# A graph network and two attention rounds on one core: the last chunk's chain is spread over 24 slots in place of 12, one pair of blocks is taken later, and VectorE makes the chunk's mean and variance

## The reference, cut to what matters

```
h = max(layernorm(x), 0);  x = x + gnn(h, adj)      # hyperbolic graph network
h = max(layernorm(x), 0);  x = x + agnn(agnn(h))    # two attention rounds

gnn:   h1 = h_mul(h, embed), bias added;  neigh = exp0(adj @ log0(h1))
       out = h_mul(concat(h, neigh), layer), bias added
agnn(x):  s = beta * (xn @ xn.T), xn = x / |x|
          s = where(adj > 0, s, -1e9);  return leaky(softmax(s) @ x)
```

## Time and profile before

| | |
|---|---|
| median of three runs | 963.98 us |
| the profiled execution, its own time | 963.64 us |
| its span | 962.0 us |
| TensorE busy | 926.9 us, 96% |
| VectorE busy | 792.5 us, 82% |
| ScalarE busy | 538.0 us, 56% |
| granted TensorE clock, mean | 0.997 of full speed |

### The profile page before, as it was taken

One profiled execution on the slowest core, in us unless ns is written; L12 is line 12 of the kernel. 1 busy time (PEld: TensorE's weight loads), 2 busy tenths in 40 slices (PEclk: granted clock), 3 DMA queues, 4 the chain that ended last, 5 costly groups with the idle time before them and its releaser, 6 DMA issues.

```text
span 962.0 us, 22931 instructions
## 1 busy us (share of the span) xinstructions
PE 926.9 (96%) x9016; PEld 692.1 (72%) x9016; DVE 792.5 (82%) x1980; ACT 538.0 (56%) x867; POOL 7.2 (1%) x20
## 2 busy tenths in 40 slices
PE   7799999999997999999999999999999999999996
PEld 6644444444445878888888888778888888888886
DVE  7874778777789887978989898998788787888888
ACT  7802222232337766657656667796575565656564
POOL 0000000000000000000000000000000000000000
PEclk9999999999999999999999999999999999999998
DMA  8368888888851555455655545545455555565631
GB/s 298 154 222 289 283 298 293 279 286 283 293 180 57 232 196 210 186 202 198 249 195 212 220 180 216 210 160 201 177 219 219 232 206 201 220 228 194 259 144 37
DMA packets 30419, 207.26 MB, mean 215 GB/s; under 512 B 3632, under 2 KB 4784, under 8 KB 5744
## 3 DMA queue, kind: packets, MB, share of 16 engines
q1 hardware_dynamic: 28752, 203.70, 58.5%
q0 software_dynamic: 560, 1.84, 0.5%
q10 hardware_dynamic: 1008, 0.33, 0.1%
HBM read 203.75 MB, written 2.10 MB: 214 GB/s over the span
## 4 chain that ended last, share of the span: by engine, by line
PE 86%; ACT 6%; DVE 5%; issue 2%; DMA 0%; DVEq 0%; ACTq 0%
PE acc_ps L496 23%; PE s_ps L649 18%; PE s_ps L635 10%; PE acc_ps L707 6%; PE acc_ps L703 6%; PE acc_ps L705 6%; PE acc_ps L680 5%; PE acc_ps L676 5%; PE acc_ps L678 5%; ACT work L1078 1%; ACT set L800 1%; DVE work L1742 1%; PE s_ps L477 1%; ACT xt L822 1%; DVE work L1750 1%
## 5 line engine op out<-in xcount | busy, mean ns | idle before, releaser
L1078 ACT ACTIVATE work<-s_ps,beta_bias,beta_scale 128x1024 f32<-128x1024 f32 x144 | 173.5, 1205 | 212.2 <-PE s_ps L649 212.2
L496 PE MATMUL acc_ps<-ring,set 128*128 128x512 f32 x512 | 222.1, 592 | 1.6 <-DVE set L1348 1.6
L1760 DVE SCALAR_TENSOR_TENSOR h_all<-ring,s_ps 128x1024 f32<-128x1024 f32 x112 | 136.6, 1220 | 65.3 <-PE s_ps L635 63.9
L496 PEld LDWEIGHTS acc_ps<-ring,set 128*128 128x128 f32 x512 | 96.2, 190 | 117.5 <-issue 115.6
L1742 DVE TENSOR_TENSOR work<-work 128x1024 f16<-128x1024 f32 x96 | 132.7, 1382 | 5.4 <-ACT work L1088 5.4
L1088 ACT ACTIVATE work<-work 128x1024 f16<-128x1024 f32 x96 | 131.5, 1370 | 3.0
L1750 DVE SCALAR_TENSOR_TENSOR work<-ring,work 128x1024 f32<-128x1024 f32 x96 | 116.9, 1218 | 0.0
L649 PE MATMUL s_ps<-xt 128*128 128x512 f16 x432 | 105.4, 379 | 4.1 <-ACT work L1078 3.3
L649 PE MATMUL s_ps<-set 128*128 128x512 f16 x432 | 105.0, 379 | 0.5 <-ACT work L1078 0.5
L703 PE MATMUL acc_ps<-src,work 128*128 128x129 f16 x576 | 102.5, 219 | 2.0 <-DVE work L1750 2.0
L707 PE MATMUL acc_ps<-src,work 128*128 128x129 f16 x576 | 102.8, 222 | 0.0
(11 more groups left out here) (279 smaller groups left out, 1737.9 us busy)
## 6 DMA issues: line engine op xcount, KB each, us to landing
ring<-in_adj_t SPq DMA_DIRECT2D x192, 1024.0 KB, 5.0
x_sb<-in_x SPq DMA_DIRECT2D x4, 512.0 KB, 7.2
out<-x_sb POOLq DMA_DIRECT2D x7, 256.0 KB, 2.7
out<-x_sb SPq DMA_DIRECT2D x1, 256.0 KB, 2.7
w<-in_layer ACTq DMA_DIRECT2D x2, 64.0 KB, 8.2
w<-in_embed ACTq DMA_DIRECT2D x1, 64.0 KB, 4.5
eb<-in_embed_bias ACTq DMA_DIRECT2D x1, 64.0 KB, 6.9
lb<-in_layer_bias ACTq DMA_DIRECT2D x1, 64.0 KB, 7.9
```

Of the source, the lines that this page charges most:

```text
L496: last = nc.tensor.matmul(agg, v_sb[:, jb, :], ring[:, k, b, :], start=jb == 0, stop=jb == NB - 1)
L1078: nc.scalar.activation(values[x.n % VR], score_ps, ACT.Exp, bias=beta_bias[:, x.la:x.la + 1], scale=beta_scale[:, x.la:x.la + 1]).then_inc ...
L1760: V.scalar_tensor_tensor(turned[x.off % MR].rearrange("p (b j) -> p b j", b=CB), ring[:, x.mir_tile % AR, :, ds(x.h * HB * P, HB * P)], 0. ...
```

## The change

Four things are changed together:
- The order of round 0's halves. `half` is now made of segments: row 0 without its last pair (halves 0 to 13), row 1 (14 to 27), then the pair of chunks 0 and 7 as (a, b) = (7, 0) (28, 29), then rows 2 to 7. Row 0's own sums leave PSUM after half 13 into the free first part of `mirror_sums` (`own_kept`, ScalarE); the late pair's mirrored sum is added to them and its own sum goes to chunk 7's part (`late_total`, VectorE). Row 0 so ends with half 29, behind row 1 (half 27). Its tiny products stand in `mirrored_sum` of the late pair. Round 1's order stays.
- A pause does two slots in place of one: the chain lies over slots 1 to 24, chunk 7's columns are turned in slot 24 and first needed by half 26.
- The sums of rows in round 0 move from slots 4 to 8, 14 and 15 to slots 18 to 23 and 27.
- Mean and variance of the last chunk come from VectorE's statistics (`chunk_stats`, behind pause 7) in place of ScalarE's two passes (`chunk_variances`); ScalarE's rectified rows and squares (`chunk_relu`) are answered behind pause 8.

```diff
@@ -289,33 +289,69 @@
...
+        Seg = namedtuple("Seg", "first last row opens_after")
...
+        def add_seg(la, a, bs, row, opens_after):
+            first = len(half)
+            for b in bs:
+                own_tile = len(tile_of)
+                tile_of.append((b, a, len(half) + 1, None))
+                if b != a:
+                    tile_of.append((a, b, len(half) + 1, off_count[0] + 1))
+                for h in range(2):
+                    off = off_count[0] if b != a else None
+                    off_count[0] += b != a
+                    half.append(Half(la, a, b, h, len(half), off, off // 2 if b != a else None, len(segs),
+                                     own_tile, own_tile + 1))
+            segs.append(Seg(first, len(half) - 1, row, opens_after))
+            return segs[-1]
+        LATE = NC - 1
+        kept_seg = add_seg(0, 0, range(LATE), None, 0)
+        seg = add_seg(0, 1, range(1, NC), 0, 1)
+        rows_of.append(Row(0, 1, seg.first, seg.last))
+        late_seg = add_seg(0, LATE, (0,), None, 2)
+        rows_of.append(Row(0, 0, kept_seg.first, late_seg.last))
+        LATE_ROW = 1
+        for a in range(2, NC):
+            seg = add_seg(0, a, range(a, NC), a, a + 1)
+            rows_of.append(Row(0, a, seg.first, seg.last))
+        for a in range(NC):
+            seg = add_seg(1, a, range(a, NC), NC + a, NC + 1 + a)
+            rows_of.append(Row(1, a, seg.first, seg.last))
...
-        LAST_CHUNK_AT = 12
-        turned_at = {LAST_CHUNK_AT: (0, NC - 1), **{rows_of[a].last + (11 if a == 5 else 10): (1, a) for a in range(NC)}}
+        late_pair = half[late_seg.first].pair
+        def flushes_before(r):
+            return max([x.pair + 1 for x in half if x.off is not None and x.la == r.la and x.b == r.a], default=0)
+        def rows_summed_to(i):
+            return i + 1 - (i >= LATE_ROW)
+        def totals_to(i):
+            return i + 2
+        LAST_CHUNK_AT = 24
+        order_of = {(r.la, r.a): i for i, r in enumerate(rows_of)}
+        turned_at = {LAST_CHUNK_AT: (0, NC - 1), **{r.last + (11 if r.a == 5 else 10): (1, r.a) for r in rows_of[:NC]}}
...
-        SUMS_AT = 2 * NC - 1
-        SUMS_AT_OF = {4: (0, 1), 5: (2,), 6: (3,), 7: (4,), 8: (5,), 14: (6,), SUMS_AT: (7,)}
+        def turn_of(la, c):
+            return order_of[0, c] if la else c
+        SUMS_AT_LA = (rows_of[0].last, LAYER + 2 * NC - 1)
+        SUMS_AT_OF = {SUMS_AT_LA[0] - 11 + i: c for i, c in {2: (0, 1), 3: (2,), 4: (3,), 5: (4,), 6: (5,), 7: (6,),
+                                                             11: (7,)}.items()}
+        SUMS_AT_OF.update({LAYER + i: c for i, c in {4: (0, 1), 5: (2,), 6: (3,), 7: (4,), 8: (5,), 14: (6,),
+                                                     2 * NC - 1: (7,)}.items()})
@@ -640,8 +677,10 @@
...
                 wait(pe, raised, x.n)
-                if x.a == 0 and x.h == 0:
-                    pe.wait_ge(xt_lo[x.la], x.b + 1)
+                if x.la == 0 and x.h == 0 and (x.a == 0 or (x.a, x.b) == (1, NC - 1)):
+                    pe.wait_ge(xt_lo[0], x.b + 1)
+                elif x.a == 0 and x.h == 0:
+                    pe.wait_ge(xt_lo[1], max(x.b, LATE_ROW) + 1)
                 for u in range(HB):
@@ -678,7 +717,9 @@
...
                         last = nc.tensor.matmul(mir_ps[:, x.h, o], w[:, WORD_LO, col], src[x.la][:, q, F:AW],
-                                                start=False, stop=ib == CB - 1)
+                                                start=False, stop=ib == CB - 1 and x.pair != late_pair)
+                    if x.pair == late_pair:
+                        last = nc.tensor.matmul(mir_ps[:, x.h, o], tiny[:, :], sums_parts, start=False, stop=True)
                 last.then_inc(mir_added, 1)
@@ -686,20 +727,20 @@
...
-                r = rows_of[x.row]
+                seg = segs[x.seg]
                 pe.wait_ge(own_made, x.n + 1)
...
                     pe.wait_ge(consts_made, 9)
-                if x.n == r.first and x.row != LAST_ROW:
-                    wait(pe, total_made, x.row)
-                own_ps = own_of(x.row)
-                if x.n % LAYER == SUMS_AT - 2:
+                if x.n == seg.first and seg.row != LAST_ROW:
+                    wait(pe, total_made, seg.opens_after)
+                own_ps = own_of(seg.row)
+                if x.n + 2 in SUMS_AT_LA:
                     pe.wait_ge(sums_copied, x.la + 1)
...
                         col, q = ds(u * CH + ib * P, P), x.b * CB + x.h * HB + u
-                        opens = x.n == r.first and u == 0 and ib % 2 == 0
+                        opens = x.n == seg.first and u == 0 and ib % 2 == 0
                         nc.tensor.matmul(own_ps[:, ib // 2, ds(ib % 2 * PW, PW)], w[:, WORD_HI, col],
@@ -904,23 +945,12 @@
...
-            def chunk_variances():
+            def chunk_relu(c):
                 asked_for()
                 for b in range(CB):
-                    last = nc.scalar.activation(t2[:, b, :], t1[:, b, :], ACT.Copy, scale=-1.0 / F,
-                                                accum_out=small[:, 3, b:b + 1])
+                    last = nc.scalar.activation(t2[:, b, :], t1[:, b, :], ACT.Relu, bias=small[:, 3, b:b + 1])
                 last.then_inc(chunk_made, 1)
                 act.wait_ge(chunk_made, 1)
-                for b in range(CB):
-                    last = nc.scalar.activation(t3[:, b, :], t1[:, b, :], ACT.Square, bias=small[:, 3, b:b + 1],
-                                                accum_out=small[:, 2, b:b + 1])
-                last.then_inc(chunk_made, 1)
-            def chunk_relu(c):
-                for b in range(CB):
-                    last = nc.scalar.activation(t2[:, b, :], t1[:, b, :], ACT.Relu, bias=small[:, 3, b:b + 1])
-                last.then_inc(chunk_made, 1)
-                act.wait_ge(chunk_made, 3)
                 for b in range(CB):
@@ -965,10 +995,8 @@
...
                 on(ACT.Tanh, sm(5, CB), sm(4, CB))
-                for i in (6, 7):
+                for i in (6, 7, 8):
                     pause(i)
-                chunk_variances()
-                pause(8)
                 chunk_relu(c)
@@ -1092,16 +1120,22 @@
...
                 wait(act, flushed, x.pair)
-                wait(act, total_made, x.la * NC)
+                wait(act, total_made, x.la * (NC + 1))
                 nc.scalar.activation(mirror_sums[:, ds(x.b * CB, CB), :].rearrange("p (k b) w -> p k (b w)", k=2),
...
             def first_total(i):
-                act.wait_ge(row_summed, i + 1)
+                act.wait_ge(row_summed, rows_summed_to(i))
                 wait(act, inverse_made, i)
...
+            def own_kept():
+                act.wait_ge(own_added, kept_seg.last + 1)
+                nc.scalar.activation(mirror_sums[:, 0:CB, :].rearrange("p (k b) w -> p k (b w)", k=2), own_ps, ACT.Copy)\
+                    .then_inc(total_made, 1)
@@ -1152,13 +1186,16 @@
...
                 first = x and x.off is not None and x.h == 1 and x.a == 0
-                if i is not None and rows_of[i].a == 0:
+                own_leaves = n - 4 == kept_seg.last or (i is not None and i == NC)
+                if n - 4 == kept_seg.last:
+                    own_kept()
+                elif i == NC:
                     first_total(i)
...
                     raise_scores(at(n))
-                if i is not None and first:
+                if own_leaves and first:
                     first_flush(x)
@@ -1173,11 +1210,12 @@
...
-                slot(i + 1)
+                for n in range(SLOTS_PER_PAUSE * i + 1, SLOTS_PER_PAUSE * (i + 1) + 1):
+                    slot(n)
...
                 last_chunk(between)
-                for n in range(PAUSES + 1, NH + 4):
+                for n in range(SLOTS_PER_PAUSE * PAUSES + 1, NH + 4):
                     slot(n)
@@ -1481,12 +1519,22 @@
...
                                                  ALU.mult, ALU.add)
-                ask(ins)
+                step(ins)
+            def chunk_stats(c):
+                for b in range(CB):
+                    ins = V.bn_stats(stats[:, b, :], t1[:, b, :])
+                step(ins)
+                V.memset(sm(0, CB), 0.0)
+                for b in range(CB):
+                    ins = V.bn_aggr(mean_var[:, b, :], stats[:, b, :])
+                step(ins)
+                V.tensor_scalar(small[:, 2, 0:CB], mean_var[:, 0:CB, 1], LN_EPS, None, ALU.add)
+                ask(V.tensor_scalar(sm(3, CB), mean_var[:, 0:CB, 0], -1.0, None, ALU.mult))
...
                 answered()
-                V.tensor_scalar(small[:, 2, 0:CB], small[:, 2, 0:CB], 1.0 / F, LN_EPS, ALU.mult, ALU.add)
-                step(V.tensor_scalar(small[:, 2, both], small[:, 2, both], TINY, None, ALU.max))
+                step(V.tensor_scalar(squares, squares, TINY, None, ALU.max))
                 inv_sqrt(sm(1, 2 * CB), squares, sm(3, 2 * CB), meanwhile)
@@ -1538,6 +1586,7 @@
...
                 pause(7)
+                chunk_stats(c)
```

(72 more changed lines are left out.)

14 lines of the change are left out of this document (7 added, 7 removed).

## The result

The changed kernel takes 966.19 us (median of 7 runs, 965.89 to 967.63), the kernel before 963.97 in the same session (7 runs, 962.91 to 964.98): ratio 1.0027, 95% interval [1.0016, 1.0038], so slower, by 2.2 us. The forecast was 965.0. The profiled execution has a span of 964.6 us (its own time 966.23), against 962.0 (963.64).

The account below looks back on a forecast made before the run. TensorE was taken as the bound, with 3.35 us of stalls between scores 6 and 13 from the last chunk's serial chain. New stalls 1.33 + 1.53 + 1.5, less 3.35, gave +1.0: 965.0 us, range 960.6 to 967.4.

Parts of the forecast that it names:

- The answers: ScalarE answers after two slots; turnings behind squares, logarithms and rectified rows late by 1.68, 1.33 and 1.53 us.
- the tangent's: Hyperbolic tangent's answer after slot 12: turning ready at T(13) + 3.99, not late.
- the 1 to 2 us named as the sign: Sign of being right: VectorE idle that long before the steps after squares, logarithms and relu, turnings late by 1.3 to 1.7.
- The sum with a further 1.38 at the logarithms: Skill's rule adds 1.38 us DRAIN to the table load: turning late by 2.71, time 966.4.
- The row ends: Rows 1 and 0 end close together: 0.95 late at slot 34, 0.55 at slot 37; together 1.5 us.
- The rival of a jam: ScalarE's 2.85 us row work in slots 33 and 35 delays exponentials: 3.8 for 1.5, time 967.3, chance 0.21.
- the 6 us that were named as its other sign: A slot near 34 longer than this would show the jam at the row ends.
- The sum from T(6) on: From half 6's scores: new stalls 1.33 + 1.53 + 1.5 = 4.4, gone 3.35, so +1.0 us.
- Up to T(6): Stage start until half 6's scores: the squares' answer gives back what the start gains, 0; T(6) = 308.97.
- The statistics: Mean and variance on VectorE behind slot 16: 1.6 us more there, ScalarE loses 2.84, nothing on the path.
- without it the relu's answer would be 2.84 later: What moving the statistics to VectorE saves: one round over ScalarE ahead of the rectified rows' answer.
- The cover works: Rival: answers fall where VectorE is behind, row ends don't jam; 3.35 and 1.0 won, 0.3 left: 959.9, chance 0.21.

Follow-up runs that it names:

- e2: Changed kernel with ScalarE giving three answers (squares, logarithms, rectified rows and squares) between the two slots of a pause, not behind both; 963.37 us, 0.9992.
- e10: Changed kernel with row 1's squares on ScalarE a slot earlier and the rest of row 0's ending three slots later; 965.50 us, 1.0016.
- e7: Changed kernel with idle products (6, 7, 5 and 10) filling all four TensorE gaps at the start of the attention; 964.35 us, 1.0005.
- e5: Kernel before with only the statistics moved to VectorE; order, pauses and row sums as before; 963.69 us, 0.9999.
- e3: Changed kernel with row 1's squares and high part on ScalarE and its first six inverse-root steps on VectorE one slot earlier; 965.43 us, 1.0023.
- e6: Changed kernel without VectorE's statistics, ScalarE's two passes with sums put back behind pause 7; 969.20 us, 1.0049.
- e11: Changed kernel with e2's early answers, e7's filled gaps and e10's spread row endings together; 959.93 us, 0.9961.
- e9: Kernel before with idle products (6, 7, 5, 8, 4) in TensorE's gaps at the start; 963.75 us, 1.0000.
- e1: Changed kernel with 20 idle products on TensorE in slot 3, overfilling the 2.48 us gap between own sum 0 and the turning; 967.51 us, 1.0048.
- e4: Changed kernel with one slot per pause and chunk 7's columns turned in slot 12, as before; new order, moved row sums and statistics stay; 967.65 us, 1.0043.
- e8: Changed kernel with e2's early answers, e7's filled gaps and ScalarE's half of e3 (row 1's squares earlier) together; 960.62 us, 0.9965.

## Why the prediction was right, and the term that was not

The forecast was 965.0 and the time is 966.19, which is slower and clear of the noise, an outcome given 0.25. The mechanism is the one that was forecast; one term of the sum was put at nothing and measured 1.5.

**The answers.** Right, place and size. VectorE goes on at T(5) + 1.68 (305.62), T(11) + 0.82 (335.89) and T(19) + 2.10 (374.27); forecast were 1.79, 0.87 and 2.22. The turnings are late by 1.58, 1.30 and 1.35 for forecast 1.68, 1.33 and 1.53, and the tangent's isn't. The offsets were read from the earlier trace rows and did not depend on the load. Two of VectorE's waits, 2.35 and 2.77, are longer than the 1 to 2 us named as the sign: the first since slot 4 was 0.95 too long, and for the second the prediction's own offsets give 3.0 (6.69 - 3.7). e2 moves nothing but the answers, and the three stalls go. The sum with a further 1.38 at the logarithms, 966.4, is nearest to the measured time, but by chance: it asks for a turning late by 2.71 there.

**The row ends.** Right: 0.96 in slot 34 and 0.74 in slot 37 (wait 0.59), forecast 0.95 and 0.55. The kernel before already pays 0.15 of the first (its slot 34 is 3.70). e10 supports the cause, two rows' work in the same slots: held apart, 1.08 come back. The rival of a jam (3.8 there, by its rows 3.88) fell by its own bound of 2.4 us of stall: it was 1.70. Slot 37 is 6.11, over the 6 us that were named as its other sign, but 5.37 of that is work, with four turned columns in it.

**The sum from T(6) on.** New 1.30 + 1.35 + 1.70 and 0.10 in slot 21, gone 3.35: +1.10. Measured are +0.82, as before had two turnings behind diagonal halves (slots 20 and 34) that cost 0.16 each and that the sum left out.

**Up to T(6).** This term failed in size: forecast "nothing is won", T(6) = 308.97; measured 310.45, a loss of 1.47. The turning ahead of scores 4 starts at 297.77, as forecast (297.9). From there the rows at low clock make the loss: T(4) is 299.43 for 298.8, slot 4 is 4.51 for 3.56 and slot 5 6.51 for 6.61, in all 0.63 + 0.95 - 0.10 = 1.48. With the clock up the sum is right: T(5) - T(0) was forecast as 20.71 (302.36 - 281.65) and is 20.73 in e7. What was left out is the granted clock: 0.50 behind the idle stretch that the sum itself had foreseen. With the gaps filled the time is 964.35, 0.65 under the forecast; without, 966.19, 1.2 over it. The page of before gave no warning, since its clock is 1.00 with gaps of 1.47, 1.62, 1.64 and 2.02 us. That it fell and that the stretch had no slack, both were needed; e5 has the first without the second, e3 has both.

**The statistics.** "Nothing on the path" is right, and "without it the relu's answer would be 2.84 later" is not: without them the own sum of half 14 waits 2.03 for a copy behind ScalarE's passes (e6), and the answer comes no later behind its scores (6.56 us after T(18) in both kernels).

**The rivals.** "The cover works", 959.9, is what e11 reaches (959.93) once answers, gaps and row ends are mended. It was a right account of what two slots for each pause offer, and a wrong one of what this code takes. That the figures agree so closely is luck: it had 1.0 for the start, where e7's start is 1.68 shorter than before's without the row sums, and 0.3 of stall left, where slot 18 alone keeps 0.53.

**Open.** Why the clock falls in one execution and not in another: e5 has before's gaps and it fell, e9 filled them. All six profiled executions of the new order with two slots per pause and a gap left unfilled (after, e1, e2, e3, e6, e10) had it fall between 288 and 304 us, none of the three filled ones did. The kernel before, filled or not (e9), and e4 had none either. The price, 1.3 to 2.8 us of start (against e7's; e1, whose filling is too long, aside), is between single executions. In e2 the single times lie from 961.21 to 964.01, in e11 from 959.38 to 960.74, which would fit a fall that comes at different places from run to run; that isn't shown. A profile shows one run only, and the mean clock of the other runs can't tell, since it takes in falls elsewhere: before's profiled execution has 0.50 behind its last matmul, e7's 0.52 at 39 to 42 us, in the first stage.

## What to carry to other kernels

When work is spread over more slots, move the answering engine's steps to the middle of the span, not to its end: an engine at 55% can still be late by 1.3 to 1.6 us each time. Where a reorder leaves TensorE idle just ahead of work that all others wait for, count its next microseconds at the lower clock as well (8 transposes 1.86 for 1.09, scores 2.42 for 1.46), or give it idle products of the gap's measured length. Two rows' work that shares slots shows as a stall on whichever engine is fuller; moving one piece mostly moved it here (e3 won 0.53 us, e8 nothing), and spreading it over more slots took most of it away (e10).

## What the runs showed of the hardware that was not expected

TensorE's granted clock goes to 0.50 (1.2 GHz) and back within a stage, behind gaps of 1.3 to 2.5 us: ahead of the fall after, the four are 1.47, 1.62, 1.30 and 2.48. In e1, e2, e3, e5 and e6 it fell at 289 us already, with only the 1.47 and the 1.62 just behind; before, after, e4 and e10 have the same two and did not fall there. The Trainium skill (TensorE: Matmul & The Clock Gate, Why this matters for your kernels) advises against long idle gaps between bursts of matmuls, since the clock falls back to half. The trace agrees with the effect, which came here behind gaps of 1.47 and 1.62 us as well, in some executions and not in others.

An idle float32 product of 128 x 128 costs 0.22 us at full clock (e1: 40 instructions in 4.68), which makes filling a gap cheap to size: 28 of them in e7 took 1.8 us off the time.
